# Graph layer on one core: SP's loads of edges, dst rows and mask wait for layer one of the next pair

## The reference

```python
h = maximum(layernorm(x), 0)                       # 12500 x 32
e_feat = concatenate([h[src], h[dst], edge_attr])  # 400000 x 96
v = relu(e_feat @ W1 + b1) @ W2 + b2               # 96 -> 64 -> 32
x_cand = segment_max(v, dst, num_segments=12500)
out = x + maximum(x_cand, h)
```

## Time and profile before

| | us |
|---|---|
| median of three timed runs | 3181.62 |
| the timed runs | 3179.7 to 3183.01 |
| span of the profiled execution | 4798.8 |
| TensorE matmul busy | 3796.5 (79%) |
| VectorE busy | 2178.1 (45%) |
| ScalarE busy | 2192.4 (46%) |
| GpSimd busy | 2386.6 (50%) |
| granted TensorE clock, mean | 0.832 |

### The profile page before, as it was taken

One profiled execution on the slowest core, in us unless ns is written; L12 is line 12 of the kernel. 1 busy time (PEld: TensorE's weight loads), 2 busy tenths in 40 slices (PEclk: granted clock), 3 DMA queues, 4 the chain that ended last, 5 costly groups with the idle time before them and its releaser, 6 DMA issues.

```text
span 4798.8 us, 56874 instructions
## 1 busy us (share of the span) xinstructions
PE 3796.5 (79%) x19778; PEld 2547.3 (53%) x19778; DVE 2178.1 (45%) x2474; ACT 2192.4 (46%) x2555; POOL 2386.6 (50%) x2523
## 2 busy tenths in 40 slices
PE   5858788778878877877887788778877887778787
PEld 3536455555555545555555555555555555555465
DVE  4211554445444444544444455444444454445356
ACT  2214454445444444544444445444544454445355
POOL 6653455555455455455545555555455555554310
PEclk8979888888778888888887888888888888888798
DMA  8700222222222222222222222222222222222112
GB/s 255 279 10 25 70 80 88 92 85 61 57 68 63 56 66 69 56 61 68 68 55 63 68 65 61 60 69 68 56 63 68 69 61 56 68 68 68 46 55 56
DMA packets 200553, 350.32 MB, mean 73 GB/s; under 512 B 73791, under 2 KB 124251, under 8 KB 200117
## 3 DMA queue, kind: packets, MB, share of 16 engines
q1 hardware_dynamic: 116638, 303.65, 18.4%
q0 software_dynamic: 80448, 41.33, 6.2%
q10 hardware_dynamic: 3332, 4.01, 0.3%
HBM read 240.36 MB, written 119.78 MB: 75 GB/s over the span
## 4 chain that ended last, share of the span: by engine, by line
PE 60%; issue 19%; another core or an unknown queue 10%; DVE 8%; ACT 2%; DMA 0%; DVEq 0%; ACTq 0%; SPq 0%
PE ps_rows L938 38%; PE ps_layers L968 8%; PE ps_layers L963 5%; DVE onehot L1250 3%; PE ps_layers L918 2%; PE ps_layers L953 2%; PE ps_layers L912 2%; DVE max_t L1318 2%; PE ps_layers L957 2%; PE ps_layers L1006 1%; DVE src_t L1285 1%; DVE rows_in L1323 1%; ACT onehot L852 0%; DVE dst_t L1305 0%
## 5 line engine op out<-in xcount | busy, mean ns | idle before, releaser
L664 POOL DMA_INDIRECT src_in<-h_dram,src_ix x2269 | 2147.7, 947 | 1951.5 <-PE ps_rows L938 976.5
L938 PE MATMUL ps_rows<-onehot,table 128*128 128x512 f32 x9898 | 2553.2, 418 | 109.0 <-issue 89.3
L938 PEld LDWEIGHTS ps_rows<-onehot,table 128*128 128x128 f32 x9898 | 1986.6, 203 | 728.8 <-issue 292.8
L852 ACT ACTIVATE onehot<-distance 128x1024 fp32r<-128x1024 bf16 x909 | 905.0, 1049 | 855.0 <-PE ps_rows L938 607.3
L847 ACT ACTIVATE distance<-picks,below_column 128x1024 bf16<-128x1024 int16 x909 | 985.1, 1139 | 0.7 <-DMA picks<-picks_dram 0.7
L838 ACT ACTIVATE hid<-ps_layers,b_col 128x512 f32<-128x512 f32 (+1 forms) x404 | 241.6, 680 | 1407.9 <-remote 912.0
L1300 DVE STREAM_TRANSPOSE ps_layers<-rows_in 128x512 f32<-128x512 f32 x202 | 133.3, 706 | 1561.3 <-ACT hid L838 1561.2
L968 PE MATMUL ps_layers<-picked_rows,w_src 128*64 128x128 f32 x1552 | 399.9, 390 | 550.1 <-issue 545.7
L1250 DVE SCALAR_TENSOR_TENSOR onehot<-picks,column,ps_layers 128x1024 fp32r<-128x1024 int16 x404 | 499.8, 1258 | 310.2 <-PE ps_rows L938 164.7
L968 PEld LDWEIGHTS ps_layers<-picked_rows,w_src 128*64 128x64 f32 x1552 | 188.8, 180 | 784.9 <-issue 782.2
L1318 DVE TENSOR_TENSOR_SCAN max_t<-mask_in,max_t,ps_layers 128x512 f32<-128x512 bf16 x196 | 249.0, 1271 | 337.2 <-remote 331.4
(11 more groups left out here) (145 smaller groups left out, 1283.1 us busy)
## 6 DMA issues: line engine op xcount, KB each, us to landing
picks<-picks_dram SPq DMA_DIRECT2D x101, 512.0 KB
first_rows<-hid SPq DMA_DIRECT2D x100, 500.0 KB
rows_in<-in_edge_attr_dram SPq DMA_DIRECT2D x96, 512.0 KB
rows_in<-first_rows SPq DMA_DIRECT2D x96, 512.0 KB
run_max<-rows_in SPq DMA_DIRECT2D x96, 512.0 KB
src_in<-h_dram,src_ix POOLq DMA_INDIRECT x2269
mask_in<-mask_dram SPq DMA_DIRECT2D x96, 256.0 KB
h_dram<-h_sb ACTq DMA_DIRECT2D x4, 392.0 KB, 5.9
```

The lines of the kernel that those rows point to most:

```text
L664: pool.indirect_dma_start(out=src_in[:, slot, g, r, :], out_offset=None, in_=rows[:, :], in_offset=bass.IndirectOffsetOnAxis(ap=src_ix[:, ...
L852: nc.scalar.activation(onehot[:, RING_AT[c] + BY_DVE[c] + k, :, :].rearrange("p g w -> p (g w)"), distance[:, k, :], ACT.Relu, bias=1.0, s ...
L938: mm = nc.tensor.matmul(ps_rows[g][side][:, 0:WIDE], table[:, i * SIDES + side, part, :], onehot[:, RING_AT[c] + t, g, :], start=(i + part ...
```

## The change

In `feed`, the load of picks comes first. Where edges, dst rows and mask of pair j + 2 are loaded by the full form (not the tail's), SP now waits for hid_summed >= (j + 2) * A ahead of them, which layer one of pair j + 1 brings. The waits that stood there stay. Since SP takes its instructions in order, indices, mask and store of pair j come after that wait too.

```diff
             def feed(j, k, turn, settled=True, loads=True, picks=True, indices=True, end=False, tail_load=False, tail_store=False, last_indices=False):
                 slot = k % 2
+                if picks:
+                    sp.wait_ge(rows_masked, j * MASKS + 2 * MASKS)
+                    sp.sem_inc(loads_begun, 1)
+                    load_picks(j + 3, 1 - slot)
+                if loads and not tail_load:
+                    sp.wait_ge(hid_summed, j * A + 2 * A)
+                    sp.sem_inc(loads_begun, 1)
                 if loads:
                     sp.wait_ge(ea_turned, j * 2 + 2)
                     sp.sem_inc(loads_begun, 1)
@@
                     sp.wait_ge(first_turned, j * 2 + 2)
                     sp.sem_inc(loads_begun, 1)
                     load_first(j + 2, slot, tail_load)
-                if picks:
-                    sp.wait_ge(rows_masked, j * MASKS + 2 * MASKS)
-                    sp.sem_inc(loads_begun, 1)
-                    load_picks(j + 3, 1 - slot)
                 if indices and k % AHEAD == IX_AT:
                     half = k // AHEAD
                     for g in range(2):
```

## The result

The changed kernel takes 4296.11 us, the median of four runs (4291.89 to 4300.99), against 3182.32 us for the kernel before on the same chip: a ratio of 1.349 with a 95% interval of 1.348 to 1.351. It is 1114 us slower. The forecast was 4050 us with a range of 3780 to 4430: right in direction and within the range, 246 us too low.

A forecast was written before the change was run, and what follows sets the result against it. The timed kernel was taken to run at TensorE's pace, about 27.3 us a pair. Late loads made the cycle 36.4 us: 94 x 9.1 = 857, plus 10 for filling, on 3181.6 gives 4050 us, range 3780 to 4430.

The forecast's parts named there:

- 26.8 us a timed cycle: Cycle of the kernel before: timed median less 666 us outside the long cycles, over 94 cycles.
- no stall in the timed kernel: Layer one's stall beside bulk transfers was taken as nearly all the profiled execution's; timed pairs take about 27.3 us.
- S + 1: S is when layer one of pair j + 1 is summed; VectorE was to want the edges about 1 us later.
- mask landed at S + 15.3: Late loads: 1.31 MB at 100 GB/s, 13.1 us, plus 1.2 to first bytes, 0.9 to semaphore, 0.1 wake-up.
- The chain behind it: VectorE's work after the mask, then TensorE's chunks 2 and 3, bringing the next layer one at S + 32.8.
- The clock term: TensorE's clock at 0.50 for some 6.5 us after its idle before chunk 2, costing 2.4 us a cycle.
- Picks first: Picks moved ahead of edges, dst rows and mask in SP's order: priced at nothing.
- The late store: Store of pair j going out last, up to a cycle later: priced at nothing.
- The filling: 1 MB more in SP's queue in ten of the first cycles, delaying picks: +-20 us, 10 taken.
- (a): Rival: TensorE's clock stays down for the cycle's whole second half; cycle 43.6 us, 4715 us in all, chance 0.08.
- (b): Rival: loads run at 265 GB/s, mask lands at S + 7.2, no change, 3182 us; chance 0.03.
- (c): Rival: timed runs stall in layer one too and the change removes it, 3088 us at 1 us a pair; chance 0.03.

The follow-up runs named there:

- e1: The kernel before, unchanged, run once more for a second profile beside a time: 3184.03 us.
- e3: The changed kernel with the wait on hid_summed asking for layer one of pair j instead of j + 1, one cycle earlier: 3182.04 us, ratio 1.000.
- e2: The changed kernel without the wait on hid_summed, so only the new order with picks first remains: 3182.04 us, ratio 1.000.
- e10: The changed kernel with edges and mask loaded ahead of the wait, dst rows alone behind it, edges and dst rows by one DMA a lane: 3208.78 us.
- e6: The changed kernel with the store of pair j issued ahead of the wait on hid_summed: 4268.01 us, ratio 1.341.
- e9: The changed kernel with edges and dst rows loaded by one DMA a lane and the mask loaded ahead of the wait: 3240.12 us, ratio 1.016.
- e7: The changed kernel with edges and dst rows loaded by four DMAs of 32 partitions instead of one of 128: 3610.05 us, ratio 1.135.

## Why the prediction was right, point by point

**The gap between profile and time.** The step read 26.8 us a timed cycle from the difference and took the undisturbed 27.3. e1 shows 28.17 on average and 27.3 in most. (27.3 from 43.97 is 16.7 us a pair, not the 16.5 of the text.) What lies outside the 94 cycles is 3182.2 - 2647.6 = 535 us, not the 666 of the disturbed execution. The conclusion that decided the sign, no stall in the timed kernel, was right.

**The mechanism.** The loads lost their cover, VectorE's chain behind the mask became the cycle, TensorE waited ahead of chunk 2, SP and VectorE waited where it said. e3 (cover back: no loss), e2 (order: nothing) and e10 (wait kept, late bytes gone: 0.7%) show it from three sides, and the table gives the slope. One reading was off without a price: the text has VectorE want the edges at S + 1, while its transposes of them begin at 4631.38 us in the cycle of the earlier trace rows, 1 us before S. That, and edges that came 1.7 us later than forecast, is why it waits 10.7 us for them and not some 6; the mask, which lands last, decides.

**The size.** Forecast 36.4 - 27.3 = 9.1 us a cycle, measured 39.93 - 28.17 = 11.76, times 94 = 1105 of the 1117 us between the two spans. (94 x 9.1 is 855 and not 857; it changes nothing.) The step that was mis-sized is "mask landed at S + 15.3": VectorE began at S + 18.5 in the cycle shown and at S + 19.1 on average, where the step meant S + 15.4. In the cycle shown, 1.3 us of the 3.1 lie ahead of the bytes: SP's edges went out at S + 0.4 and no rate much above the gathers' own showed before 2421 us, 2.2 us after the issue, where I had 0.1 + 1.2 for both. The rest is the rate. The 100 GB/s were read with the gathers not taken off, as the rows of this kernel show: 16 GB/s for gathers alone and 112 for loads with gathers leave some 96. Nor did that hold to the end: from the landing of the edges (2427.49) to VectorE's start behind dst rows and mask (2436.95) are 9.5 us for 786 KB, 83 GB/s, where the step had 7.9 us. What lowers it stays open. It is not the store behind the mask, which e6 takes away; picks flow beside these loads (267 GB/s in all at 2430 us), and no run takes the picks away. By the Trainium skill, "DMA: Bandwidth & Descriptors", 4 engines of 27 GiB/s give 116 GB/s, and the transfer would have been 11.3 us as an estimate, 1.8 us further off than the 13.1 of the step; the runs show the lower rate.

**The chain behind it** was right: from VectorE's start to the next layer one 17.1 us on average, forecast 17.4 (5.2 to chunk 2 and 12.15 for chunks 2 and 3), and layer one 3.64. The clock term in it was right in price only. Charged was a slow stretch as long as the idle, 6.5 us, costing 2.4. In the cycle shown the clock is 0.50 from about 2435.2 to 2445.5 us (0.65 and 0.73 in the stretches of 1 us at its two ends), 10 us, longer than TensorE's 9.5 us of idle, and only 3.4 us of it lie on work; in the cycle before it was 5.6. The 42 matmuls, 9.7 us at full clock, took 11.3 and 12.4. A longer stretch that begins sooner happened to leave about as much on work: luck.

**What was costed at nothing.** Picks first: nothing, by e2. The late store: 0.3 us a cycle, by e6. The late picks: ScalarE waits for them, which the text had not foreseen; e6 halves that wait and store and picks together give back 0.3, while the other half has no run of its own. The filling was charged with 10 us: the first 14 cycles are longer than 14 of the later ones by 10 us in the change and by 28 in e1, so it adds nothing to the loss.

**The rivals.** (a) did not come: the clock is 0.87 on average over the cycle. (b) named the point from which there is no loss, all landed at S + 7.2: the real loads miss it by 11 us, and e9 and e10, at S + 7.3 and S + 5.3, sit on it. It was a price for 265 GB/s, which the loads come near when cut by lane (240 to 262). (c) falls with e1. The changed kernel's profiled span was forecast near 4090 us and is 4299.0: lower than the earlier trace rows, while the time is higher, as the text warned.

## What to carry to other kernels

Set the span of a profile beside the timed median before pricing a stall from it, and where they differ look for an undisturbed cycle: here a stall of 16 us a pair stood in one execution only. Price a delayed load by the moment when its last consumer has it, against the slack up to a named point (S + 7.2 here), and let everything behind that point go through the in-order engine's whole queue. A wait costs nothing by itself: the same line was worth 0.7% or 35%, by how much of what stood behind it landed in time, and nothing when it asked for one cycle earlier.

## What the runs showed of the hardware

Loads of 512 KB with a dimension of 4 in front moved at about 83 to 96 GB/s, at a share of about a third with gathers, and four loads of 128 KB with 32 in front at 240 to 262 GB/s, at 0.43 to 0.56 us of SP's time for each. This fits the Trainium skill, "DMA: Bandwidth & Descriptors", section "Why a DMA increments its semaphore by 16 and not by 1", by which the slowest dimensions decide how many engines take part; the same page's rules for kernel authors advise against two transfers to disjoint halves of the partitions, because both would use all 16 engines anyway, a reason that this shape does not give (e7: 686 us gained from four parts). And one execution of the kernel before was slowed by 51%, with matmuls 0.7 us apart while transfers ran, which neither its second profile nor a timed run shows; why is open.
